# Joining the front stage and the edge stage of a graph and expert kernel into one block

## What is computed

```
h      = x_flat @ W_gat                      # 16 numbers for each node
e      = leaky_relu(a_src[src] + a_dst[dst]) # for each edge and each head
alpha  = segment_softmax(e, dst)
agg    = segment_sum(h[src] * alpha, dst)    # 16 numbers for each node
scores = layernorm(agg + b).reshape(.., heads, experts).mean(heads)
out    = x + sum over the top 2 experts of softmax(scores) * (gelu(x@W1+b1)@W2+b2)
```

## Time and profile before

| what | value |
|---|---|
| median of 3 runs | 3045.78 us (3042.99 to 3047.26) |
| the profiled execution | 3043.94 us |
| its span in the trace | 3041.6 us |
| busy: PE, DVE, ACT, POOL | 1772.9, 2257.7, 1155.3, 1864.0 us |
| mean granted TensorE clock | 0.793 of full speed |
| sort done (keys written by SP from) | 1206.35 us |
| front ends (DVE L919) | 1590.4 us |
| first gather of edge rows | 1596.56 us |

### The profile page before, as it was taken

How to read it: one execution, slowest core, us unless ns; L and a number is a source line. 1 busy time by engine, 2 the same in 40 slices (tenths; PEclk the granted TensorE clock), 3 DMA queues, 4 the chain that set the end, 5 groups by cost and what they waited for, 6 DMA issues and landing times. The chain is left out here.

```text
span 3041.6 us, 31102 instructions
## 1 busy us (share of the span) xinstructions
PE 1772.9 (58%) x8831; PEld 1218.4 (40%) x8831; DVE 2257.7 (74%) x4431; ACT 1155.3 (38%) x2319; POOL 1864.0 (61%) x1723
## 2 busy tenths in 40 slices
PE   0777774058888884466863265546554664555445
PEld 0665653045565553355761133223322332333223
DVE  7999998899999999787843655665566555655566
ACT  2676773234444442365941122222222222222222
POOL 4702244835454553477767777777777777777771
PEclk9898885589999997688956677777777777777777
DMA  5698000111111111222121122112211222122211
GB/s 217 210 354 323 17 22 15 34 34 39 33 47 37 52 32 37 72 57 69 34 41 29 39 45 43 33 41 45 43 34 40 44 45 43 31 43 45 43 31 36
DMA packets 170129, 192.34 MB, mean 63 GB/s; under 512 B 59241, under 2 KB 126096, under 8 KB 169008
## 3 DMA queue, kind: packets, MB, share of 16 engines
q1 hardware_dynamic: 107616, 118.69, 11.7%
q0 software_dynamic: 57088, 62.48, 10.1%
q10 hardware_dynamic: 5328, 9.97, 0.9%
HBM read 91.70 MB, written 105.25 MB: 65 GB/s over the span
## 5 line engine op out<-in xcount | busy, mean ns | idle before, releaser
L1582 POOL DMA_INDIRECT edge_rows<-node_table,edge_ids x1024 | 996.2, 973 | 313.3 <-issue 296.6
L1207 POOL DMA_INDIRECT token_results<-arena,token_of x160 | 258.5, 1616 | 291.8 <-ACT arena L1141 220.9
L634 DVE TENSOR_TENSOR sort_ping<-sort_pong 128x1024 f32<-128x1024 f32 (+1 forms) x232 | 395.1, 1744 | 7.4 <-ACT sort_pong L1077 2.7
L1705 PE MATMUL x_b_featT<-ident,x_feat 128*128 128x128 f32 x128 | 34.8, 427 | 623.1 <-PEq L1304 623.1
L634 DVE TENSOR_TENSOR sort_pong<-sort_ping 128x1024 f32<-128x1024 f32 (+1 forms) x230 | 390.3, 1738 | 7.3 <-ACT sort_ping L1077 2.2
L1200 POOL DMA_INDIRECT slots<-arena,send x128 | 186.7, 1458 | 306.2 <-ACT arena L1099 272.3
L1452 DVE TENSOR_TENSOR win_score<-win,masked 128x320 f32<-128x320 f32 x64 | 28.7, 490 | 443.3 <-DMA win<-edge_table,win_ids 442.0
L1711 PE MATMUL x_b_hid<-x_featT,x_w 128*128 128x512 f32 x512 | 309.2, 758 | 28.1 <-PEq L1304 28.1
L1718 PEld LDWEIGHTS x_b_res<-x_w,x_hid 128*128 128x128 f32 x2048 | 245.3, 196 | 97.1 <-issue 97.1
L1705 PEld LDWEIGHTS x_b_featT<-ident,x_feat 128*128 128x128 f32 x128 | 22.9, 217 | 628.5 <-issue 628.5
L1718 PE MATMUL x_b_res<-x_w,x_hid 128*128 128x128 f32 x2048 | 270.2, 287 | 0.0
(11 more groups left out here) (367 smaller groups left out, 4064.4 us busy)
## 6 DMA issues: line engine op xcount, KB each, us to landing
edge_table<-zeros SPq DMA_DIRECT2D x8, 5120.0 KB, 36.2
edge_rows<-node_table,edge_ids POOLq DMA_INDIRECT x1024
arena<-slots SPq DMA_DIRECT2D x40, 260.0 KB, 2.6
slots<-zeros SPq DMA_DIRECT2D x2, 5120.0 KB, 24.4
edge_table<-edge_rows SPq DMA_DIRECT2D x64, 160.0 KB, 2.1
out_dram<-x_y ACTq DMA_DIRECT2D x33, 256.0 KB, 4.2
x<-in_x_dram SPq DMA_DIRECT2D x4, 2048.0 KB, 18.4
adjacent<-in_adj_dram SPq DMA_DIRECT2D x32, 256.0 KB, 2.7
```

The lines of the kernel that those rows point to most:

```text
L634: step(dve.tensor_tensor(vb[:, :, t, :], va[:, :, 0, :], va[:, :, 1, :], op))
L1207: pool.indirect_dma_start(rows_dram, bass.IndirectOffsetOnAxis(token_of[:, n % 4, r:r + 1], 0), res[:, n % 2, r, :], None, bounds_check=TO ...
L1582: pool.indirect_dma_start(rows[:, u, c, :], None, table_dram, bass.IndirectOffsetOnAxis(ids[:, u, c:c + 1], 0)).then_inc(rows_in[u], 16)
```

## The change

Five things change:

1. There is one `Block` for both stages. `renew_semaphores` with its two barriers goes. POOL clears and frees, at a point in `front` behind the write of the keys, the semaphores that are done by then (`early`), so that the second stage can use them.
2. The second stage is ordered by semaphores: DVE posts `known` with `found` (L919). PE, SP, and ACT wait for it, DVE and ACT wait for `tabled` too. POOL waits for `tabled` alone, gathers part 0, and only then waits for `known`, draws its constants and gathers part 1. SP loads the first ids in `front`. `edge_ids`, `edge_rows` and `wide` now lie in the memory of `sort_ping`.
3. `dve_biased` moves from behind `dve_scores`, for group n + 3, to the head of the step, for group n + 2.
4. The sort advances in every step of the tail of attention 0, so in three more steps (n = 34, 36, 38).
5. Every entry of `TURNS_AFTER` moves two half-steps ahead.

```
+        early = [att0.normed, att0.turned, ... , *rows_in, *w_in, sent_normed, *sent]
-        TURNS_AFTER = {2: (0, 1, 2, 3), 11: (4,), 12: (5, 6, 7), 21: (8,), 22: (9, 10, 11), 31: (12,), 32: (13,), 33: (14,), 34: (15,), 43: (16,),
-                       44: (17,), 45: (18,), 46: (19,), 55: (20,), 56: (21,), 58: (22,), 59: (23,), 68: (24,), 69: (25,), 71: (26,), 73: (27,)}
+        TURNS_AFTER = {0: (0, 1, 2, 3), 9: (4,), 10: (5, 6, 7), 19: (8,), 20: (9, 10, 11), 29: (12,), 30: (13,), 31: (14,), 32: (15,), 41: (16,),
+                       42: (17,), 43: (18,), 44: (19,), 53: (20,), 54: (21,), 56: (22,), 57: (23,), 66: (24,), 67: (25,), 69: (26,), 71: (27,)}
-        block = ctx.enter_context(nc.Block())
@@ DVE, loop of attention 0
-                if n <= GROUPS + 1 or n % 2:
-                    advance(2 if n > GATED and n % 2 == 0 and n <= GROUPS else 1)
+                advance(2 if n > GATED and n % 2 == 0 and n <= GROUPS else 1)
@@ DVE, loop of attention 1
             for n in range(-3, GROUPS + 1):
+                att1.dve_biased(dve, n + 2)
                 att1.dve_held(dve, n - 1)
                 att1.dve_scores(dve, n + 2)
-                att1.dve_biased(dve, n + 3)
                 att1.dve_updated(dve, n - 1)
...
                     link(dve.tensor_reduce(counted, tiles[:, :], AX_X, ALU.add))
+                    dve.sem_inc(ids_s, 1)
...
-            dve.scalar_tensor_tensor(found[:, 0, :], rows_f, float(FAN), counts[:, :], ALU.mult, ALU.add)
+            dve.scalar_tensor_tensor(found[:, 0, :], rows_f, float(FAN), counts[:, :], ALU.mult, ALU.add).then_inc(known, 1)
@@ SP, front
             sp.wait_ge(ids_out, 16)
+            sp.wait_ge(ids_s, 2)
+            ids_v = ids_dram.rearrange("r (h q c) -> (r h) q c", c=PART_TILES, q=P)
+            for u in (0, 1):
+                sp.dma_start(ids[:, u, :], ids_v[u]).then_inc(ids_in[u], 16)
@@ POOL, front
             pool.wait_ge(keys_out, 16)
+            free_semaphores(early)
             pool.wait_ge(ranked_s, 1)
@@ second stage, DVE
+            dve.wait_ge(known, 1)
+            dve.wait_ge(tabled, tables)
             link(dve.memset(due[:, :], 0.0))
@@ second stage, POOL
+            pool.wait_ge(tabled, tables)
+            gather(0)
+            pool.wait_ge(known, 1)
             pool.affine_select(out=column_end[:, :], in_=ones[:, :], compare_op=ALU.is_ge, fill=0.0, base=-(P - 1),
...
             pool.iota(pref_i[:, :], [[-1, E]], base=E, channel_multiplier=0).then_inc(drawn, 1)
-            gather(0)
             gather(1)
@@ second stage, SP
-            for u in (0, 1):
-                sp.dma_start(ids[:, u, :], ids_v[u]).then_inc(ids_in[u], 16)
+            sp.wait_ge(known, 1)
@@ second stage, ACT and PE
+            act.wait_ge(known, 1)
+            act.wait_ge(tabled, tables)
+            pe.wait_ge(known, 1)
@@ build
+        ping = keep("sort_ping", [P, COLS])
+        ids = ping[:, 0:2 * PART_TILES].bitcast(U32).rearrange("p (u c) -> p u c", u=2)
+        edge_rows = ping[:, 2 * PART_TILES:2 * PART_TILES * (1 + ROW)].rearrange("p (u c w) -> p u c w", u=2, c=PART_TILES)
+        block = top.enter_context(nc.Block())
-        renew_semaphores()
```

More of the change, by code:

```diff
@@ L439, in front @@
 def front(nc, sem, a, x, x_in, stats, scratch, rstd, shift, masked, tab, W, fills, ident, ones, upto, row_id, wanted, counted, found,
-          keys_dram, slots_dram, rows_dram, edges_dram, ids_dram, table_dram):
+          keys_dram, slots_dram, rows_dram, edges_dram, ids_dram, table_dram, block, ping, ids, ids_in, known, free_semaphores):
     with ExitStack() as ctx:
@@ L1220, in _, with edges_and_experts1 @@
                                             bass.IndirectOffsetOnAxis(row_ids[:, q:q + 1], 0)).then_inc(fetched_s[n % FETCHED], 16)
-def edges_and_experts1(nc, sem, a, x, rstd, shift, node, found, counted, source_ids, row_id, table_dram, edges_dram, out, ident, ones):
+        return tabled, 16 * (GROUPS // CHUNK)
+def edges_and_experts1(nc, sem, a, x, rstd, shift, node, found, counted, source_ids, row_id, table_dram, edges_dram, out, ident, ones, block, ping, ids, rows, ids_in, rows_in, known, tabled, tables):
     E = TOP_EXPERTS
```

52 lines of the change are left out of this document (26 added, 26 removed).

## The result

The changed kernel takes 3021.32 us (median of 4 runs, 3019.23 to 3023.74) beside 3046.24 for the kernel before (4 runs): a ratio of 0.9926 with a 95% interval of 0.9914 to 0.9938. It is faster by 22.5 us by that ratio and by 24.9 us by the two medians, where 28.5 were forecast. The profiled execution took 3023.74, the slowest of the four; its span is 3021.7, against 3041.6 before, so 19.9 us shorter.

The account below looks back on a forecast made before the run. POOL's unbroken chain of indirect DMAs was taken to bound the second stage, so an earlier first gather ends it earlier: 30.0 - 1.5 = 28.5 us, from 3045.78 to 3017.3, range 3010 to 3031.

Parts of the forecast that it names:

- One block: At the hand-over: with the other edits, first gather at 1566.6 instead of 1596.56, 30.0 us sooner; constants on POOL's path cost 1.5.
- Later bias: Attention 1 up to 1449 us: DVE's 26.8 us of waits for PE's right side go; 24 us taken as saved.
- Behind 1449 us I count no gain: Late attention 1: no gain counted, since ACT is busy 82.25 and PE 81.71 of 95 us there.
- the forecast holds while the bias saves at least 17 us: Hand-over: POOL is ready 7 us after the landed table, so POOL sets the first gather if the bias saves 17 us.
- POOL's 9.8 us of waiting go too: POOL's fetches: with DVE 20 us earlier, the 9.8 us of waits for DVE's counts vanish; the fetches end at 1572.2.
- Fuller tail: Tail of attention 0: three more sort pieces slow POOL's sends, 2.0 us each, so experts 0 start 5.9 us later.
- Turns two half-steps ahead: Experts' stage: PE reaches the first turn 10.7 us sooner, less 5.9; the sort ends 5.9 us earlier, at 1200.4.
- the late table's bias: Rival at the hand-over: bias gains only 8 or 0 us, so the table ends the wait; 3027 or 3035; chance 0.15.
- The sort wins nothing: Rival in tail and experts: slower sends delay experts 0 by 12 us or more, sort ends as before; 3023; chance 0.08.
- That sends don't slow down: Rival in the tail, from the skill's rule: no delay, sort ends 11.8 us earlier, sum 34.4; 3011; chance 0.08.
- POOL never stood for `known`: Rival behind part 0's gathers: POOL waits 25 us for `known` or the plan, nearly no gain; 3043; chance 0.03.
- The gathers kept their mean: Rival in the second stage: all 1024 gathers get dearer; at 50 ns each, 3068; chance 0.03.

Follow-up runs that it names:

- the three kernels above: Changed kernel with old tail and turns plus unread one-input or two-input DVE work (one execution each), and with old turns only (3034.15 us, 0.9966); fetches 332.2 to 333.5 us.
- the second trace: The changed kernel run and profiled once more with no edit: 3019.47 us (5 runs), ratio 0.9917 against the kernel before.
- the kernel with both undone: Changed kernel with the old tail of attention 0 and the old table of turns, block and bias kept: 3024.56 us (6 runs), ratio 0.9935 against the kernel before.
- the first trace: The first profiled execution of the changed kernel: 3023.74 us, span 3021.7 us.

## Why the prediction was right, and where its sizes were off

The mechanism is right: the second stage is a chain of POOL's DMAs that keeps its length, and the change moves its start. The edits work in the way named, its signs at the hand-over came true (no wait for counts, none for `known`, first gather 0.3 us behind the last fetch, first wait for windows 30.7 us), and 3021.3 lies in the range. Its signs of size did not: the fetches take 334.7 us and not 329, the sort ends at 1204.5 and not 1200, the first gather comes at 1575.9 and not 1567. The sizes went as follows.

*One block.* In the trace before, 14.2 us more than the issue lay between last fetch and first gather (1582.03 to 1596.56, less 0.3 us); after, none. As forecast in size, but the prediction reads the stretch as `found` and then 3.3 us of barriers and clearing. The last to arrive was POOL's drain, at 1591.3, which it doesn't have; that the whole stretch went is right for the changed kernel, where POOL leaves no block there. The constants cost 1.4 us ahead of part 1, the stage grew by 0.7 and 0.3 us instead of 1.5, within its spread.

*Later bias.* This is the term that was mis-sized most: 24 us were taken and 13.2 to 16.3 saved. Up to 1440 us the step is close, with 19.5 to 22.7 us gained. What failed is "Behind 1449 us I count no gain": nothing was put where 6 us are lost again, as PE's projection and ACT's root and exponentials became the next releasers. I had looked for waits of DVE before the edit; they were small because DVE waited elsewhere first. The prediction named the condition itself, "the forecast holds while the bias saves at least 17 us", and it was not met. With 13.2 to 16.3 the table's last part is issued some 328 us behind the first fetch, lands 5.2 us later and lets POOL go 0.8 behind that: about 334 us, against the 329 at which POOL was to be ready.

The second term is "POOL's 9.8 us of waiting go too". They went, and 5.2 us came back as dearer fetches, so that the fetches take 334.7 us. The two errors don't add up. Had the fetches cost nothing more, the table would have held POOL until about 334 us, as in the three kernels above; so 5 of the 6 us that are missing in this stretch would be missing by the bias alone, and the dearer fetches add the last one.

*Fuller tail.* "Each piece costs POOL 2.0 us, three cost 5.9": 6.6 and 6.8 us in one course, 8.7 and 9.0 in the other. The mechanism is that of the prediction, and the send rows are its rows; what was missing is that a send that starts just behind a piece's start takes up to 3.0 us, so that a third of a microsecond at its start decides over 2.2.

*Turns two half-steps ahead.* "10.7 + 1.1 - 5.9 = 5.9" holds in the second trace: 728.5 - 721.8 = 6.7 us, 6.0 against the kernel with both undone. In the first trace it is 1.4 and 0.7: the phase of sort and turns is not "the old one" there, as the clock falls at other places. The medians, 3 to 5 us, lie between the two courses.

In us gained against the trace before, from the columns of the table of kernels, the forecast and the two traces after stand as follows. The medians lie between the traces: 24.9 us, and 25.7 when measured again. That the second trace comes so near to the forecast is partly luck: 2.3 us of it lie ahead of every edit, and the turns' 6.7 make up for a part of what the fetches lack.

| step | forecast | first trace | second trace |
|---|---|---|---|
| up to the root (same program) | 0 | 1.0 | 2.3 |
| root to first fetch | 5.9 | 1.4 | 6.7 |
| the fetches | 9.8 | 4.0 | 4.5 |
| last fetch to first gather | 14.3 | 14.2 | 14.2 |
| second stage | -1.5 | -0.7 | -0.3 |
| sum | 28.5 | 19.9 | 27.4 |

Of the rivals, the late table's bias (a gain of 8, or 0) was nearer in size than my 24, and it came within 1.1 us: the table was not the releaser in the changed kernel, but it was in three kernels that differ from it ahead of the fetches only. "The sort wins nothing" describes the first trace and not the second. That sends don't slow down is refuted by their rows (only plain DMAs don't, as shown above), and POOL never stood for `known`. The gathers kept their mean, 973 ns.

## What to carry to other kernels

Where two chains meet, price an edit on one of them only against the other: the block and the bias alone gave 7 and 9 us by the times (6.6 and 3.8 by the first gather), together 20 (18.6). When an edit removes a wait, list what the waiting engine needs next in the same step and expect part of the wait back there (27 of 38 us here), and expect that indirect DMAs of GpSimd beside it may get dearer (2% here). Ask of every barrier which engine reaches it last: here it was the one whose DMAs were thought to be done. Work put in a gap of VectorE beside a queue of GpSimd's indirect DMAs is not free; short instructions there cost little, those of 2.3 us double a DMA.

## What the runs showed of the hardware

- An indirect DMA's issue on GpSimd took 0.97 us alone, 0.97 to 1.04 beside 0.49 us instructions of VectorE with one input, 1.14 to 1.37 beside 0.69 us instructions with two, and mostly 1.90 to 2.99 beside 2.29 us instructions with two. A plain DMA's issue took 0.56 to 0.61 beside the same 2.29 us instructions.
- At the end of a block GpSimd's drain ended 9.2 us behind the end of its last indirect DMA, in two kernels, and held the barrier.
- One program has two courses that differ by 5.3 us in the same stretch and agree within 0.2 us among themselves (721.8 twice, 727.1 and 727.3). They part at a start that differs by a third of a microsecond; later the granted clock is 0.82 in one where the other has 1.00, and then 0.60 and 0.71 in the other where the one has 0.83 and 1.00.
- Executions of the same program differ by up to 3 us ahead of the edits, at the root (511.8 to 514.9), so terms of a few us are read from differences within a trace and not from its absolute times.
